# Expert tiles of a routed LSTM layer: the first two tiles' columns made by products with tables of ones, the last tile's rows added by weighted products

## The chip, the cores and the metric

One core of a Trainium2 chip runs the whole program. The time is the device time of one execution in microseconds (us), lower is better. The number compared is the median over runs.

## The reference, cut to what matters

The network has four layers over 625 nodes with 512 features, each a graph part, an attention part and a feed-forward part. The change touches only the last feed-forward part, a mixture of 8 experts of which each row (node) uses 2. Each expert is an LSTM whose sequence has one step here, so it starts from a zero state:

```python
xn = layernorm(x)                                 # 625 x 512
logits = xn @ router_w + router_b                 # 625 x 8
top_vals, top_idx = top_k(logits, 2)
rw = softmax(top_vals, axis=1)                    # two weights a row
for e in range(8):                                # for the rows that chose e
    i, g, o = split(xn @ Wi[e] + b[e])            # the forget gate meets a zero cell
    c = sigmoid(i) * tanh(g)
    y_e = (sigmoid(o) * tanh(c)) @ Wo[e] + bo[e]  # 512 x 512
x = x + sum over the two chosen experts of rw * y_e
```

## The kernel before, in words

All five engines and the DMA queues run one hand-ordered program. PSUM is split into 4 slots of two banks; `TILES` (line 146 and after) gives the order in which TensorE fills them and says which engine empties each ("A" ScalarE, "V" VectorE). `begin` (line 814) makes TensorE wait until the tile four before has been emptied. `full`, `evacd` and `made` are waits on semaphores: a tile filled, a tile emptied, a value made.

**Routing.** VectorE normalises the rows (L1771), TensorE transposes them, five row blocks of 125 rows (`turn_rows`, L855), ScalarE copies them out (L1440), and `router` (products on L824) makes the logits. VectorE adds the bias (L1959), subtracts the maximum (L1963), waits for ScalarE's exponential (L1487), and picks the two best experts (`pick2`, L1928 to L1944). TensorE counts the rows per expert with a triangular table and tables of ones (L1364, L1366, L824, float32: two records per product in the profile). From the counts (read at L2517) VectorE works out for every row its two slots in a list sorted by expert, in which each expert starts on a multiple of 128. The list has EX = 17 tiles of 128 slots, of which each belongs to one expert.

**Filling the tiles.** POOL fetches one weight table by an indirect DMA (L790, 1 MB each: "i", "g", "o" for the three gates and "y" for the output), then writes each row block of xn twice, to its slots in `rows_by_expert` (L797, 10 scatters of 256 KB), then fetches the other tables. Three sets of four tables fit at a time. SyncE waits for all ten scatters, then loads tile 0 and tile 1 (L617). TensorE transposes tile 0 (L1381), VectorE copies it out (L2556). Beside this TensorE transposes the combine weights (L970) and multiplies them with the output biases (L824, 8 rows by 512 columns), and VectorE adds that to X (L2552).

**The loop over 17 tiles.** For tile j TensorE does, in this order: gate i of tile j (a bias product of 24 rows in bf16, L1389, and 4 float32 products of 512 columns, L1393, two records each), the transposes of the hidden rows of tile j-1 (L1400), gate g, the output rows of tile j-1 (L824), the transposes of tile j+1 (L1381), gate o. ScalarE applies sigmoid and tanh, VectorE multiplies and copies (L2568, L2575, L2562). SyncE stores the output rows to `expert_rows` (L620; the last two tiles on L623).

**The end.** When all 17 stores have landed, POOL gathers each row block's two outputs (L807, 10 gathers). VectorE adds them to X, weighted (L2581, L2584), and SyncE writes the result (L627).

## Time and profile before

| | |
|---|---|
| median of three runs | 4341.97 us (4341.44 to 4346.38) |
| the profiled execution, its own time | 4356.8 us |
| its span in the profile | 4354.6 us |
| granted TensorE clock, mean | 0.959 |
| busy: TensorE, VectorE, ScalarE, POOL | 4111.0, 2294.4, 1870.3, 456.7 us |
| the chain that ended last, by engine | TensorE 92%, VectorE 5%, others 1% or less |

Times in the rows are microseconds from the start of the span. A row of the timeline gives start, length, engine, line, operation, output and input, and in brackets the idle time before it and what ended it. Busy time is that of all instructions of an engine in a stretch, overlaps counted once; "PEclk" is the clock that TensorE was granted, 1.00 for 2.4 GHz and 0.50 for 1.2 GHz. "PEld" is the load of the stationary operand. Everything described above begins at about 3990 and is over at 4354.6.

### The profile page before, as it was taken

How to read it: one execution, taken by the hardware profiler on the slowest of the kernel's cores; microseconds unless marked ns; L12 is line 12 of the kernel's file. 1: busy time of each engine (PE TensorE's matmuls, PEld its weight loads, DVE VectorE, ACT ScalarE, POOL GpSimd, SP SyncE). 2: the span in 40 equal slices, each digit the busy share in tenths (PEclk: the TensorE clock that was granted, in tenths of full speed). 3: DMA queues.
4: the chain of work that ended last, by engine and by line, in shares of the span. 5: the costliest groups of instructions: out<-in, count | busy, mean ns of one | idle time of the engine just before them, and what ended most of it. 6: DMA issues, size and time to landing. Idle time of an engine off the chain costs nothing.

```text
span 4354.6 us, 138764 instructions
## 1 busy us (share of the span) xinstructions
PE 4111.0 (94%) x53867; PEld 2286.2 (53%) x53867; DVE 2294.4 (53%) x10677; ACT 1870.3 (43%) x7114; POOL 456.7 (10%) x450
## 2 busy tenths in 40 slices
PE   9888899899999999999999999999999998986897
PEld 7445445455555544456788744434444575455343
DVE  6323512666666666666666666656665153454111
ACT  0010102377777655577777655555554142120111
POOL 0010000100000033100000033201231000011221
PEclk9998899999999999999999999999999998996898
DMA  3000110451000000000000000000000150101874
GB/s 117 17 32 26 39 46 29 146 168 37 10 0 0 1 2 2 5 0 0 0 0 0 1 2 2 5 0 1 2 1 9 58 125 23 65 25 28 328 296 149
DMA packets 65464, 195.72 MB, mean 45 GB/s; under 512 B 30024, under 2 KB 37903, under 8 KB 49387
## 3 DMA queue, kind: packets, MB, share of 16 engines
q0 software_dynamic: 25744, 105.19, 7.6%
q1 hardware_dynamic: 39613, 89.02, 6.2%
q8 instruction: 78, 1.28, 0.1%
q14 instruction: 29, 0.24, 0.0%
HBM read 159.74 MB, written 34.15 MB: 45 GB/s over the span
## 4 chain that ended last, share of the span: by engine, by line
PE 92%; DVE 5%; ACT 1%; issue 1%; POOL 1%; DMA 1%; POOLq 0%; DVEq 0%; ACTq 0%
PE PS L1107 51%; PE PS L824 23%; PE PS L1393 4%; PE PS L1101 3%; PE PS L910 3%; PE PS L1165 2%; PE PS L855 1%; PE PS L1243 1%; PE PS L1293 1%; PE PS L1233 1%; PE PS L1223 1%; ACT BUF L1440 0%; DVE stats L1754 0%; PE PS L883 0%; PE PS L1389 0%
## 5 line engine op out<-in xcount | busy, mean ns | idle before, releaser
L1107 PE MATMUL PS<-BUF,ls_hid 128*1 128x256 f32 x40000 | 2323.0, 379 | 4.8 <-DVE ls_hid L2183 4.7
L1107 PEld LDWEIGHTS PS<-BUF,ls_hid 128*1 128x1 f32 x40000 | 1112.9, 83 | 1004.2 <-DVE ls_hid L2183 289.3
L2153 DVE STREAM_TRANSPOSE ls_turn<-PS 128x192 f32<-128x192 f32 x1250 | 479.2, 383 | 466.9 <-PE PS L1107 466.6
L1559 ACT ACTIVATE ls_th<-ls_pr 128x1 f32<-128x1 f32 x2500 | 601.0, 287 | 102.1
L824 PE MATMUL PS<-ring,BUF 128*125 128x512 f32 (+1 forms) x1120 | 480.6, 588 | 19.5 <-DVE BUF L1895 5.8
L2183 DVE SCALAR_TENSOR_TENSOR ls_hid<-ls_gate,ls_th 128x1 f32<-128x1 f32 x2500 | 345.9, 149 | 233.7 <-ACT ls_th L1559 214.6
L1552 ACT ACTIVATE ls_gate<-ls_turn 128x6 f32<-128x6 f32 x1250 | 265.6, 212 | 319.4 <-DVE ls_turn L2153 239.4
L824 PEld LDWEIGHTS PS<-ring,BUF 128*125 128x125 f32 x1120 | 211.0, 191 | 275.2 <-issue 255.6
L1440 ACT ACTIVATE BUF<-PS 128x500 f32<-128x500 f32 (+1 forms) x100 | 50.8, 562 | 619.7 <-PE PS L855 619.5
L2158 DVE STREAM_TRANSPOSE ls_turn<-PS 128x64 f32<-128x64 f32 x1250 | 279.2, 223 | 0.1
L2164 DVE SCALAR_TENSOR_TENSOR ls_pr<-ls_gate 128x4 f32<-128x4 f32 x1250 | 215.5, 172 | 112.1 <-ACT ls_gate L1552 4.1
L1101 PE MATMUL PS<-BUF,picked 126*1 126x256 bf16 (+1 forms) x5000 | 263.1, 272 | 8.7 <-ACT picked L1569 6.9
L1569 ACT ACTIVATE picked<-pick 128x1 bf16 x624 | 128.5, 206 | 298.4 <-PE PS L1107 277.8
L1554 ACT ACTIVATE ls_gate<-ls_turn 128x2 f32<-128x2 f32 x1250 | 255.7, 205 | 0.2 <-DVE ls_turn L2158 0.2
L2169 DVE SCALAR_TENSOR_TENSOR ls_c<-ls_pr 128x2 f32<-128x2 f32 x1250 | 200.5, 160 | 42.6
L2174 DVE TENSOR_SCALAR ls_gate<-ls_c 128x2 f32<-128x2 f32 x1250 | 217.6, 174 | 0.0
L1564 ACT ACTIVATE BUF<-ls_hid 128x4 f32 x625 | 130.8, 209 | 192.0 <-DVE ls_hid L2183 192.0
L732 POOL DMA_INDIRECT edges_by_cell<-duo x80 | 94.5, 1181 | 890.1 <-DVE ls_turn L2153 887.0
L824 PE MATMUL PS<-BUF,ring 128*128 128x113 f32 (+1 forms) x640 | 181.2, 444 | 2.3 <-ACT BUF L1440 1.4
L1101 PEld LDWEIGHTS PS<-BUF,picked 126*1 126x1 bf16 (+1 forms) x5000 | 124.2, 84 | 98.5 <-ACT picked L1569 7.9
L855 PE MATMUL PS<-ident,BUF 125*128 125x125 f32 x390 | 65.0, 336 | 96.1 <-DVE BUF L1771 80.9
L1165 PE MATMUL PS<-AH,rows 125*32 125x512 bf16 (+3 forms) x2560 | 155.6, 297 | 0.0
(384 smaller groups left out, 3601.9 us busy)
## 6 DMA issues: line engine op xcount, KB each, us to landing
cell_bias<-BUF SPq DMA_DIRECT2D x5, 2441.4 KB
BUF<-cell_bias POOLq DMA_DIRECT2D x5, 2441.4 KB, 14.9
gate_inputs<-BUF SPq DMA_DIRECT2D x5, 1344.0 KB
rows_by_expert<-BUF POOLq DMA_DIRECT2D x1, 4352.0 KB, 29.7
BUF<-rows_by_expert SPq DMA_DIRECT2D x17, 256.0 KB, 7.0
expert_rows<-BUF SPq DMA_DIRECT2D x17, 256.0 KB, 2.3
BUF<-in_L_wh SPq DMA_DIRECT2D x4, 1024.0 KB, 12.6
ring<-in_L_w SPq DMA_DIRECT2D x4, 1024.0 KB, 4.8
```

Source lines behind the costliest of these rows:

```text
L824: ins = nc.tensor.matmul(out, a, b, start=(j == 0), stop=(j == len(terms) - 1))
L1101: nc.tensor.matmul(ls_sum[u][f][32 * q:32 * q + 1, :], picked[0:k, :], gx_tile[g][0:k, q, 2 * f:2 * f + 2, :, :].rearrange("p u j n -> p j ...
L1107: ins = nc.tensor.matmul(ls_sum[u][f][32 * q:32 * q + 1, :].rearrange("p (j n) -> p j n", j=4), ls_hid[:, c:c + 1], ls_half[:, q, c, :, f, :],
L1165: ins = nc.tensor.matmul(PS[p:e, 1, a:b], m[:, p:e], hot_rank[u][:, a:b], start=False, stop=False, skip_group_check=True)
L1552: nc.scalar.activation(ls_gate[:, f, 0:6], ls_turn[:, f, 2:8, 0], ACT.Tanh).then_inc(ls_sig[f], 1)
L1554: nc.scalar.activation(ls_gate[:, f, 8:10], ls_turn[:, f, 0:2, 0], ACT.Tanh).then_inc(ls_out_gate[f], 1)
L1559: nc.scalar.activation(ls_th[:, f, c:c + 1], ls_pr[:, f, c:c + 1], ACT.Tanh, scale=0.5, bias=ls_pr[:, f, 2 + c:3 + c]).then_inc(ls_tanh[f], 1)
L2153: V.transpose(ls_turn[:, f, 2:8, :], ls_sum[u][f][:, 64:256].rearrange("p (g n) -> p g n", g=6)).then_inc(ls_turned[f], 1)
L2158: V.transpose(ls_turn[:, f, 0:2, :], ls_sum[u][f][:, 0:64].rearrange("p (g n) -> p g n", g=2)).then_inc(ls_turned_o[f], 1)
L2164: V.scalar_tensor_tensor(ls_pr[:, f, :], ls_gate[:, f, 0:4], 1.0, ls_gate[:, f, 4:8], ALU.add, ALU.mult).then_inc(ls_prod[f], 1)
L2174: V.tensor_scalar(ls_gate[:, f, 6:8], ls_c[:, f, :], 0.5, None, ALU.mult).then_inc(ls_state[f], 1)
L2183: V.scalar_tensor_tensor(ls_hid[:, 2 * f + c:2 * f + c + 1], ls_gate[:, f, 8 + c:9 + c], 1.0, ls_th[:, f, c:c + 1], ALU.add, ALU.mult).the ...
```

## The change

Five things are altered, all in the last feed-forward part, except for one more blank DMA at the program's start.

1. The router's products are interleaved with the last transposes, and VectorE no longer waits for the exponential before picking.
2. The counts are made in bf16 (0 and 1 are exact), the total counts first.
3. The columns of tiles 0 and 1 no longer come from memory: VectorE compares an iota of 256 columns with each row's two slots, and TensorE multiplies xn by these tables of ones (20 products of 256 columns). The ten scatters stay, for tiles 2 to 16.
4. POOL fetches tables i0, g0, o0 and i1 ahead of the scatters, and g1, y0, o1, y1 behind them.
5. Tile 16's rows are not stored and gathered. Its rows in `expert_rows` are blank from the start, and a weighted table of ones (VectorE, transposed on TensorE) multiplies tile 16's rows in PSUM, in one accumulation with the bias products, which move here from ahead of the loop. POOL's gathers wait only for the stores of tiles 0 to 15.

The core of the diff:

```diff
+                pool.dma_start(ys_d[128 * (EX - 1):128 * EX, :], blank).then_inc(pad_out, 16)
-                pool.wait_ge(ex_routed, 1)
-                fetch("i", 0)
-                pool.wait_ge(ex_routed, 2)
+                pool.wait_ge(ex_ready, 1)
+                for q, j in (("i", 0), ("g", 0), ("o", 0), ("i", 1)):
+                    fetch(q, j)
+                pool.wait_ge(ex_ready, 2)
                 for i in range(2 * NT):
                     pool.indirect_dma_start(xs_d, ...xn[:, i % NT, :], None).then_inc(ex_scattered, 16)
+                for q, j in (("g", 1), ("y", 0), ("o", 1), ("y", 1)):
+                    fetch(q, j)
+                for j in range(2, EX):
...
-                pool.wait_ge(ex_stored[0], 16 * (EX // 2 + 1))
+                pool.wait_ge(ex_stored[0], 16 * (EX // 2))
...
+            def turn_and_route(turned, stage, ready, which, n):
+                for t in range(NT):
+                    if t == NT - 1:
+                        route_row(stage, 0, turned, which, n)
+                    o = begin(turned, t)
+                    ready(t)
+                    for c in range(KC):
+                        ins = nc.tensor.transpose(...)
+                    ins.then_inc(tile_full, 1)
+                for t in range(1, NT):
+                    ins = route_row(stage, t, turned, which, n)
+                ins.then_inc(tile_full, 1)
...
-                nc.tensor.matmul(o[0:R, 0:8 * NT], ltri, hots.rearrange("p t e -> p (t e)"), start=True, stop=False)
+                mm_all(o[:, 512:520], [(ones16, hots16[:, t, :]) for t in range(NT)])
+                nc.tensor.matmul(o[0:R, 0:8 * NT], ltri, hots16.rearrange("p t e -> p (t e)"), start=True, stop=False)
...
+                o = begin("L3f.xa", 0)
+                pe.wait_ge(*made("L3f.place"))
+                for c in range(KC):
+                    ins = mm_all(o[:, 256 * c:256 * c + 256],
+                                 [(xn[:, t, 128 * c:128 * c + 128], ex_first[:, t, :]) for t in range(NT)])
+                ins.then_inc(tile_full, 1)
...
                 for j in range(EX + 1):
                     if j < EX:
-                        pe.wait_ge(*evacd(f"L3f.x{j}"))
+                        pe.wait_ge(*(evacd(f"L3f.x{j}") if j > 1 else evacd("L3f.xa") if j else (ex_ready, 4)))
                         gate("i", j)
...
+                    if j == EX - 2:
+                        turn_probs("L3f.cT", sm[:, 0, :, :], 8)
+                        pe.wait_ge(ex_ready, 5)
+                        o = begin("L3f.pT", 0)
+                        for t in range(NT):
+                            ins = nc.tensor.transpose(o[:, 128 * t:128 * t + R], ex_last[:, t, :], ident[0:R, 0:R])
+                        ins.then_inc(tile_full, 1)
+                for t in range(NT):
+                    o = begin("L3f.b", t)
+                    nc.tensor.matmul(o[0:R, 0:D], combT[:, t * R:(t + 1) * R], eb[:, 0, :], start=True, stop=False)
+                    if t == 0:
+                        pe.wait_ge(*evacd(f"L3f.y{EX - 1}"))
+                    nc.tensor.matmul(o[0:R, 0:D], ex_lastT[:, t * R:(t + 1) * R], ex_y[(EX - 1) % 2],
+                                     start=False, stop=True).then_inc(tile_full, 1)
...
+                for t in range(NT):
+                    st.done(V.tensor_scalar(ex_first[:, t, :], iota[0:R, 0:256], r_slot[:, t:t + 1], None, ALU.is_equal))
+                for t in range(NT):
+                    ins = V.scalar_tensor_tensor(ex_first[:, t, :], iota[0:R, 0:256], r_slot[:, NT + t:NT + t + 1],
+                                                 ex_first[:, t, :], ALU.is_equal, ALU.add)
...
+                dve.wait_ge(*full("L3f.xa", 0))
+                V.tensor_copy(ex_xT[0], both[:, 0, :, :]).then_inc(ex_ready, 1)
+                took(V.tensor_copy(ex_xT[1], both[:, 1, :, :]), "L3f.xa", 0)
+                dve.wait_ge(*evacd("L3f.xa"))
+                for t in range(NT):
+                    for k, dst in enumerate((ex_last, ex_last2)):
+                        at = NT * k + t
+                        st.done(V.tensor_scalar(dst[:, t, :], iota[0:R, 0:128], r_late[:, at:at + 1], r_w[:, at:at + 1],
+                                                ALU.is_equal, ALU.mult))
+                st.after()
+                V.tensor_tensor(ex_last, ex_last, ex_last2, ALU.add).then_inc(ex_ready, 1)
...
                 for t in range(NT):
                     dve.wait_ge(ex_back[t], 32)
+                    for k in range(2):
+                        st.done(V.scalar_tensor_tensor(Xr[:, t, :], ex_got[:, k, t, :], ...))
+                        st.after()
+                    dve.wait_ge(*full("L3f.b", t))
+                    took(V.tensor_tensor(Xr[:, t, :], bank("L3f.b", t)[0:R, :], Xr[:, t, :], ALU.add), "L3f.b", t)
```

## Rows read from the trace of the kernel before

**Rows 1.** Busy time of each engine in three stretches; columns as on the first line.
```profile
core 0: us, PE busy (x) PEld busy (x) DVE busy (x) ACT busy (x) POOL busy (x), PEclk, DMA share, GB/s
4013.00:4043.00 30.00, 8.45 (x10) 2.65 (x9) 4.48 (x12) 0.81 (x1) 23.20 (x22) 0.50 0.78 242
4046.00:4053.00 7.00, 7.00 (x10) 2.63 (x11) 0.00 (x0) 0.37 (x1) 0.14 (x1) 0.57 1.02 421
4073.00:4300.00 227.00, 227.00 (x606) 99.85 (x605) 38.24 (x58) 40.73 (x70) 50.12 (x53) 1.00 0.70 276
```

**Rows 2.** Timeline of the routing, from the router's products to the reading of the counts.
```profile
3995.53 6.89 PE L824 MATMUL PS<-wr,BUF 128*125 128x8 f32 x40 [0.73 <-ACT BUF L1440]
...
4003.49 0.20 DVE L1928 TENSOR_REDUCE smr<-sm 125x5 f32<-125x40 f32 x1 [0.30 <-ACT sm L1487]
...
4006.06 0.20 DVE L1944 TENSOR_TENSOR sm<-sm 125x40 f32<-125x40 f32 x1
...
4008.45 2.28 PE L824 MATMUL PS<-sm,ones 125*128 125x8 f32 x10
...
4010.84 0.22 DVE L2517 TENSOR_TENSOR duo<-PS,iota 128x40 f32<-128x40 f32 x1 [3.66 <-PE PS L824]
```

**Rows 3.** Timeline from the slots to the last scatter and the second table.
```profile
4013.29 0.17 DVE L2544 CAST duo<-duo 125x10 uint32<-125x10 f32 x1
...
4013.41 1.05 POOL L790 DMA_INDIRECT BUF<-in_L_table_i,duo  x1 [27.63 <-DVE duo L2540]
...
4028.23 1.18 POOL L797 DMA_INDIRECT rows_by_expert<-BUF,duo  x1 [0.31 <-issue]
4029.71 0.98 POOL L790 DMA_INDIRECT BUF<-in_L_table_g,duo  x1 [0.30 <-issue]
```

**Rows 4.** Chain of waits, the first gate and pieces of the loop's first turn: start, length.
```profile
4045.93 6.66 PE PS L1393 x8
...
4056.54 0.44 PE PS L1381 x4
...
4060.92 0.32 PE PS L1389
4061.24 3.63 PE PS L1393 x8
```

**Rows 5.** Busy time in two stretches, for the granted clock; columns as in rows 1.
```profile
3993.00:3995.00 2.00, 1.80 (x12) 1.56 (x10) 0.00 (x0) 1.75 (x4) 0.00 (x0) 0.76 0.00 0
...
4017.00:4020.00 3.00, 3.00 (x5) 1.29 (x4) 0.97 (x3) 0.00 (x0) 2.39 (x3) 0.50 0.67 227
```

**Rows 6.** Groups by shape: count, busy us, mean ns of one, idle before.
```profile
L1059 PE MATMUL PS<-duo,BUF 128*125 128x256 f32 x20 | 4.6, 383 | 1.8 <-DVE duo L2053 1.8
L1389 PEld LDWEIGHTS PS<-BUF,duo 24*128 24x128 bf16 x51 | 4.6, 91 | 20.5 <-issue 20.5
L1786 DVE TENSOR_SCALAR BUF<-iota,ids 125x625 bf16<-125x625 f32 x80 | 44.4, 555 | 0.0
L1994 DVE SCALAR_TENSOR_TENSOR BUF<-BUF,sm 125x256 f32<-125x256 f32 x5 | 2.1, 425 | 0.2
```

**Rows 7.** DMA issues at 4013.4, 4028.2, 4029.7 and 4042.3; last number us to landing.
```profile
BUF<-in_L_table_i,duo POOLq DMA_INDIRECT x1, 5.6
...
rows_by_expert<-BUF,duo POOLq DMA_INDIRECT x1, 7.2
...
BUF<-in_L_table_g,duo POOLq DMA_INDIRECT x1, 9.1
...
ring<-in_L_table_y,duo POOLq DMA_INDIRECT x1, 24.1
```

**Rows 8.** Chain of waits at the end: the last store, first gather, last block's first sum.
```profile
4327.94 2.02 DMA expert_rows<-BUF
...
4330.48 1.22 POOL BUF L807
...
4350.33 0.76 DVE X L2581
```

**Rows 9.** Timeline, VectorE's copy of the output rows of tile 15.
```profile
4315.07 0.69 DVE L2562 COPY BUF<-PS 128x512 f32<-128x512 f32 x1 [2.11 <-PE PS L824]
```

More of the change, by code:

```diff
@@ L161 @@
         TILES += [(f"L3f.o{_j}", 1, "A", 8)]
+    if _j == EX - 2:
+        TILES += [("L3f.cT", 1, "A", 8), ("L3f.pT", 1, "A", 8)]
+TILES += [("L3f.b", NT, "V", 8)]
 MADE = [
@@ L612, in _ @@
             sp.wait_ge(ex_scattered, 16 * 2 * NT)
-            for j in range(EX + 1):
+            for j in range(2, EX + 2):
                 if j < EX:
-                    if j >= 2:
+                    if j >= 4:
                         sp.wait_ge(*full(f"L3f.x{j - 2}", 0))
@@ L965, in router, with route_row @@
                 ins.then_inc(tile_full, 1)
+            def turn_and_route(turned, stage, ready, which, n):
[5 more added lines that the diff above has]
+                    for c in range(KC):
+                        ins = nc.tensor.transpose(o[:, c * R:(c + 1) * R], xn[:, t, 128 * c:128 * c + 128], ident[0:R, 0:R])
+                    ins.then_inc(tile_full, 1)
+                for t in range(1, NT):
+                    ins = route_row(stage, t, turned, which, n)
+                ins.then_inc(tile_full, 1)
+            def route_row(stage, t, turned, which, n):
+                o = begin(stage, 0) if t == 0 else slot(stage, 0)
+                pe.wait_ge(*evacd(turned, t))
+                return mm_all(o[0:R, n * t:n * t + n], [(xnT[:, c, t * R:(t + 1) * R], wr[:, which, c, 0:n])
+                                                        for c in range(KC)])
             def turn_probs(stage, a, n):
@@ L1721, in _ @@
                         expert_gate("o", j, ex_o, ACT.Sigmoid)
+                    if j == EX - 2:
+                        copy_probs("L3f.cT", 8)
+                        act.wait_ge(*full("L3f.pT", 0))
+                        took(nc.scalar.activation(ex_lastT.rearrange("p (t n) -> p t n", t=NT),
+                                                  slot("L3f.pT", 0)[:, 0:640].rearrange("p (t n) -> p t n", t=NT)[:, :, 0:R],
+                                                  ACT.Copy), "L3f.pT", 0)
         @block.vector
@@ L2543, in _ @@
                 st.after()
-                V.tensor_copy(ex_at, r_slot).then_inc(ex_routed, 1)
-                V.tensor_scalar(ex_pick[:, 0:EX], r_expert[0:24, :], lane8[0:24, :], None, ALU.is_equal).then_inc(ex_routed, 1)
+                V.tensor_copy(ex_at, r_slot).then_inc(ex_ready, 1)
+                for t in range(NT):
+                    st.done(V.tensor_scalar(ex_first[:, t, :], iota[0:R, 0:256], r_slot[:, t:t + 1], None, ALU.is_equal))
+                for t in range(NT):
+                    st.after(st.n - NT + 1)
+                    ins = V.scalar_tensor_tensor(ex_first[:, t, :], iota[0:R, 0:256], r_slot[:, NT + t:NT + t + 1],
+                                                 ex_first[:, t, :], ALU.is_equal, ALU.add)
+                    if t < NT - 1:
+                        st.done(ins)
+                    else:
+                        make(ins, "L3f.place")
+                V.tensor_scalar(ex_pick[:, 0:EX], r_expert[0:24, :], lane8[0:24, :], None, ALU.is_equal).then_inc(ex_ready, 1)
                 for k in range(2):
                     st.done(V.tensor_tensor(r_pick[:, k, :, :], comb, sm[0:R, 2 + 3 * k, :, :], ALU.mult))
+                st.done(V.tensor_scalar(r_late, r_slot, -128.0 * (EX - 1), None, ALU.add))
                 st.after()
                 st.done(V.reduce_sum(r_w, r_pick.rearrange("p k t e -> p (k t) e"), AX_X))
-                for t in range(NT):
-                    dve.wait_ge(*full("L3f.b", t))
-                    took(V.tensor_tensor(Xr[:, t, :], bank("L3f.b", t)[0:R, :], Xr[:, t, :], ALU.add), "L3f.b", t)
+                st.after()
                 def turned_x(j):
```

85 lines of the change are left out of this document (39 added, 46 removed), and 5 rows, old and new, of tables (MADE, TILES).

## The prediction

> **What bounds it now.** Read first the busy time by stage [rows 1]: TensorE fills every microsecond of 4073 to 4300, the loop over the 17 expert tiles, but of the 30 us ahead of its first product it is busy 8.45, at half clock, and the first gate's 7 us also run mostly at half (mean 0.57). So the loop is a block of fixed length. This change can only move its start and shorten what follows its end. Then the timeline [rows 2, 3] and the chain of waits [rows 4] show what sets the start: router products until 4002.42, two dozen 0.2 us steps of VectorE, the counts, 10 scatters issued by POOL one after the other, the last at 4028.23, its landing 7.2 us later [rows 7], the load of the rows and their transposes; the first gate's last product ends at 4045.93 + 6.66 = 4052.59. At the end [rows 8, 9] the last tile goes to memory, then POOL issues 10 gathers 1.5 us apart, and the last sum can start only at 4350.33, 19.85 us after the first issue.
>
> A difference under 0.2% (8.7 us) counts as no change.
>
> **The routing.** (a) The router now interleaves with the last transposes: TensorE's 0.73 us of idle time ahead of it goes [rows 2]: 0.7. (b) VectorE does not wait for the exponential before it looks for the maxima: the 0.30 us [rows 2] falls to the usual 0.03: 0.27. The wait moves behind the choice of experts, where the exponential is 2 us old. (c) The counts. Before: VectorE starts its mask sum at 4006.06 and can read the counts at 4010.84. The 10 records with tables of ones take 2.28 us, 0.23 each, and there are 20 such records, since float32 takes two a product. In bf16 it is 10 records; a bf16 weight load of 128 columns takes 0.09 [rows 6], at half clock I take 0.11, so 1.15 us, 0.1 ahead and 0.25 behind: the counts can be read 0.2 + 1.5 = 1.7 us after the mask sum starts, instead of 4.78. Gain 3.1. The combine weights (four steps of 0.2 us) fit beside that, so nothing is exposed. Bounds: 1.5 if the small products cost as much as now each, 3.4 if the pass is free. Sum of (a) to (c): 4.1 us.
>
> **The first tile.** Before, scatter, load, transpose. Now the slots stand ready at 4013.46 - 4.1 = 4009.36 [rows 3] and VectorE builds the table: 5 comparisons of 256 columns (a comparison of 625 against the iota takes 0.555, so 0.3 each; 1.5) and 5 comparisons with a sum (256 columns, two inputs: 0.425 to 0.46 [rows 6]; 2.3). Ready at 4013.2, TensorE at 4013.3. Then 20 products of 256 columns in float32, two records each; a record at mostly full clock takes 0.23 [rows 6], so 9.2 us at full and 18.4 at half clock. The engine comes out of idle time, so how long it stays at half decides. The transposes of this stage were already above half in the window 3993 to 3995, some 2.5 us after their start at 3991 [rows 5], the first gate only at 4052, 6.7 us after its start. I take the middle, 4.6, each costing half: 9.2 + 2.3 = 11.5, between 10.4 and 12.6. Products end at 4024.8; VectorE copies tile 0 first (0.1 + 0.7), gate 0 starts at 4025.7. If the clock holds over that 0.9 us gap, the gate's last product ends 0.32 + 3.63 later [rows 4], at 4029.6, against 4052.59: **23.0 us**. If the clock falls in the gap, 1.7 less, and with the table 0.8 us quicker, as much more. What needs weights: POOL now issues four tables first (4009.3, then 1.28 apart as its rows at 4029.71 and after), the first landing 5.6 us after issue [rows 7], the others 2.8 apart: 4015, 4018, 4020, 4023, all ahead of need. VectorE's new 11 operations (the last tile's weighted table, 3.5 us in all) stand between the two copies and the first cell product, which waits for gates 0 that end 8 us later: nothing.
>
> **The second tile and the loop.** The transposes of tile 1 leave the loop: -0.44 [rows 4]. In its last but one turn come the weights' transposes and those of the last tile's table, 5 each, 0.11 each at full clock: +1.1. Their copies on ScalarE (an estimate of 0.7 each, by VectorE's copy of 128x512 in 0.69 [rows 9]) stand ahead of gate 16's, which ends 4 us later; hidden by that gate, and 1.4 us if it were gone. Net +0.7.
>
> **The tail.** Gathers no longer wait for tile 16's store but for tile 15's. VectorE copies tile 15 at 4315.07 to 4315.76 [rows 9]; with the store's 2.02 and the 0.52 to the first issue [rows 8] POOL starts at 4318.3 instead of 4330.48, 12.2 us earlier. The last pair has landed at 4318.3 + 19.85 = 4338.2. Two sums (0.76 each [rows 8], 1.54 with the gap) and the new addition from PSUM (0.7 like the copy [rows 9], and a signal) end at 4340.5, against 4350.33 + 1.54 = 4351.87: **11.4 us**. The products that replace the load stay just inside: tile 16's copy ends at 4327.92; from there, per row block, 2 records of 8 rows and 2 of 128, 512 columns, 0.454 each (an eighth of 3.63): 1.8 us at full clock, so block 4 is there at 4336, wanted at 4339.7. Slack 3.6. VectorE before that: 2.3 us a block from 4327.9, never the later one. The five additions of the bias to X ahead of the loop lay beside the scatters; their going brings nothing. The blank written at the program's start and three small fills lie beside 100 us of TensorE: nothing.
>
> Here a rule and a row part. The row: from 4017 to 4020 TensorE was busy without a break, with products of 8 rows, and the granted clock stayed at 0.50 [rows 5]. In the tail half the records are of that kind. The Trainium skill, TensorE: Matmul & The Clock Gate, Part 1, says that sustained activity of the engine releases the throttle, and names no kind of product that would not count. By the rule the tail's products run at full clock and the sum stands; by the row they could run at half and block 4 would come at 4343.5, and the sum would be 3.8 smaller. I keep full clock, because the other half of the records fills all 128 rows.
>
> **Sum.** 23.0 - 0.7 + 11.4 = 33.7 us. The profiled execution took 4356.8 (span 4354.6 and 2.2 around it): 4323.1. It stands 14.8 above the median of 4341.97; the same difference gives **4308**.
>
> **Rivals.** (A) The queue. Scatters now stand behind three more tables than before. The rows: g0, issued at 4029.71, landed 9.1 later at 4038.8, and the eleventh after the first table, issued at 4042.26, 24.1 later at 4066.4 [rows 3, 7]: they land in order of issue, 2.76 us apart over ten steps. The last scatter is issued at 4027.9, about as now, since 4.1 us won meet 3.85 us of three more issues. If it lands at 4035.4 as now, g1 comes at 4038.9 (needed 4042.2), y0 at 4042, i2 at 4050.8 (needed 4053.7): slack 3 us. Three tables ahead are 8.3 us of transfer against 4.1 us of earlier start and the 22% of the DMA engines' time left free from 4013 to 4043 [rows 1], 6.6 us: just absorbed. If not, up to 4 us go: 4309 to 4312. Chance 0.15. The Trainium skill, DMA: Bandwidth & Descriptors, Queues, rings and completion order, has each engine take its descriptors in ring order, which is what makes this a rival and not a sharing; by it the tables of tile 1 cannot overtake a scatter, and the same 4312 is its worst case. The order of landing above agrees. (B) The tail's products at half clock: 4312, chance 0.12. For it the row at 4017; against it the 128-row half. (C) The new products do not warm the clock, whatever in them were to blame: 18.4 us instead of 11.5, and the gate starts cold (+2.7): 9.6 us lost, 4318, chance 0.06. (D) The other side: the added weight loads and small transposes, or the earlier start, leave the loop at half clock. The place is 4073 to 4300, now at 1.00 throughout [rows 1]. A tile is four times 8 records (14.5 us at 3.63), two or three sets of transposes and three bias products, some 16 us of work, and as much is lost if it runs at half clock. It decides from 34 us of loss, a little over two tiles; three would give 4308 + 48 = 4356. Nothing in the trace ran busy at half for so long with 128-row products. Chance 0.02. (E) The change doesn't do what it says, the first gate still waiting for the scatters through some semaphore: only the tail and the routing gain, 4326; by the code gate 0 waits for the copy alone. Chance 0.01.
>
> **The numbers.** The forecast has 0.64: 4308, of its own from 4305 (clock up early, 1.1; quick table, 0.8; quick counts, 0.3) to 4311 (clock up late 1.1, a fall in the gap 1.7). With A and B and the spread of 5 us between the runs of before the range is 4303 to 4316; C, D, E and what exceeds it are under 2 in 10. Faster by over 0.2%: all but D and a margin, 0.96; within 0.2%: 0.02; slower: 0.02.
>
> **What would show it.** Right: counts read 1.7 us after the mask sum; 40 records of 256 columns in 10.4 to 12.6 us; gate 0 at 4025 to 4027 at clock 1.0 and no pause of TensorE up to gate 2; the first gather at about 4296 (4318.3 less the 22.3 us by which the loop ends earlier); the last sum ready 22 us after the first gather. Wrong: TensorE waiting for a table or for tile 2's rows in the first two turns (A), a wait of VectorE for the last block's products (B), 18 us of new products (C).

## The result, and the profile of the kernel after

The change makes the kernel faster: 4309.11 us (median of 4 runs, 4308.24 to 4320.32) against 4343.32 us (median of 4, 4341.44 to 4346.38) in the same job, a ratio of 0.9927 (95% interval 0.9912 to 0.9943). In a second job (that of runs 9 to 11) the two medians were 4320.08 us (6 runs) and 4353.01 us (11 runs), and the ratio was again 0.9927 (0.9916 to 0.9939). The prediction was 4308 us, in a range of 4303 to 4316. One execution of the kernel before (4841.92 us, mean clock 0.828) and one of run 6 (14719.01 us, mean clock 0.383) were in a slow state and are in none of the ratios.

| | before | after |
|---|---|---|
| the profiled execution, its own time | 4356.8 us | 4308.24 us |
| its span | 4354.6 us | 4306.5 us |
| granted TensorE clock, mean | 0.959 | 0.968 |
| busy: TensorE, VectorE, ScalarE, POOL | 4111.0, 2294.4, 1870.3, 456.7 us | 4099.4, 2298.7, 1869.9, 458.9 us |
| start of the last row normalisation | 3990.38 | 3977.83 |
| from there to the end of the span ("the stretch") | 364.22 us | 328.67 us |

The two spans differ by 48.1 us, and this isn't the change. 12.55 us of it stand ahead of the last row normalisation, in stages that are the same in both programs. These stages show two levels. The granted clock over 3450 to 3500 is 0.76 in some executions and 0.90 in others, and those at 0.76 reach the last normalisation 9 to 13 us later. Both levels occur with the same program: a second profile of the kernel after (run 11) was at 0.76, began its last normalisation at 3990.93 and had a span of 4319.6 us, 35.0 less than the kernel before at the same level. Its stretch was again 328.67 us; spans are printed to 0.1 us. So kernels are compared here by the stretch: 364.22 - 328.67 = **35.55 us** gained, where the prediction's sum was 33.7. The medians differ by 34.2 us in the first job and by 32.9 in the second.

Where it went, by stages, each from the start of the last normalisation or the end of the stage before:

| stage | before | after | gained | predicted |
|---|---|---|---|---|
| to the CAST of the slots | 22.91 | 16.95 | 5.96 | 4.1 |
| to the end of gate 0 | 39.30 | 19.30 | 20.00 | 18.9 |
| the loop, to the copy of tile 15 | 262.48 | 263.11 | -0.63 | -0.7 |
| the tail | 39.53 | 29.31 | 10.22 | 11.4 |

The timeline of the kernel after, from the normalisation to gate 0. The columns are as in the timelines of before, to which it answers [rows 2, 3]:

```profile
3977.83 2.37 DVE L1817 TENSOR_SCALAR BUF<-X,mv,nw 125x512 f32<-125x512 f32 x5
3978.52 3.31 PE L982 MATMUL PS<-ident,BUF 125*128 125x125 f32 x16 [19.37 <-DVE BUF L1817]
...
3982.93 4.95 PE L832 MATMUL PS<-wr,BUF 128*125 128x8 f32 x32
...
3987.98 0.20 DVE L2005 TENSOR_TENSOR sm<-PS,rows 125x40 f32<-125x40 f32 x1 [7.78 <-PE PS L832]
...
3991.12 0.20 DVE L1990 TENSOR_TENSOR duo<-sm 125x40 bf16<-125x40 f32 x1
...
3991.42 0.27 PE L832 MATMUL PS<-duo 125*128 125x8 bf16 x5 [3.55 <-issue]
...
3991.66 0.57 PE L1391 MATMUL PS<-duo 125*125 125x32 bf16 x4
...
3992.33 0.22 DVE L2565 TENSOR_TENSOR duo<-PS,iota 128x40 f32<-128x40 f32 x1
...
3994.78 0.17 DVE L2592 CAST duo<-duo 125x10 uint32<-125x10 f32 x1
...
3996.23 2.05 DVE L2597 SCALAR_TENSOR_TENSOR BUF<-iota,duo,BUF 125x256 f32<-125x256 f32 x5
...
3998.43 10.59 PE L832 MATMUL PS<-BUF 125*128 125x256 f32 x40 [6.21 <-DVE BUF L2597]
...
4010.08 0.37 PE L1415 MATMUL PS<-BUF,duo 24*128 24x512 bf16 x1 [1.05 <-DVE BUF L2623]
4010.38 3.70 PE L1419 MATMUL PS<-BUF 128*128 128x512 f32 x8
...
4013.74 1.63 POOL L804 DMA_INDIRECT rows_by_expert<-BUF,duo  x1 [0.30 <-issue]
...
4015.67 0.98 POOL L796 DMA_INDIRECT BUF<-in_L_table_g,duo  x1 [0.30 <-issue]
```

Gate 0 (L1415 and L1419) starts 1.05 us after the first tiles' products, and waits for the copy alone. The last scatter is issued only while gate 0 runs, at 4013.74. From the mask sum (L1990) to the reading of the counts (L2565) it is 1.21 us, where it was 4.78 [rows 2]. The busy time of the same kernel by stretch answers to [rows 1, 5]: columns as there, PEclk the third number from the end.

```profile
3979.00:3981.40 2.40, 2.40 (x13) 2.40 (x12) 1.20 (x3) 1.29 (x3) 0.00 (x0) 0.50 0.00 0
3981.50:3984.80 3.30, 3.30 (x33) 3.30 (x32) 0.00 (x0) 1.55 (x3) 0.00 (x0) 1.00 0.00 0
3985.00:3988.00 3.00, 2.87 (x14) 2.78 (x14) 0.02 (x1) 0.00 (x0) 0.00 (x0) 0.50 0.00 0
3998.40:4001.90 3.50, 3.47 (x8) 2.86 (x9) 0.56 (x5) 0.00 (x0) 2.58 (x4) 0.50 0.92 382
4002.00:4009.00 7.00, 7.00 (x33) 5.84 (x31) 0.00 (x0) 0.00 (x0) 5.75 (x5) 1.00 0.99 374
4014.00:4280.00 266.00, 266.00 (x711) 117.05 (x711) 43.17 (x65) 49.57 (x85) 61.97 (x65) 1.00 0.72 287
4287.60:4298.20 10.60, 10.56 (x21) 2.89 (x20) 7.18 (x10) 0.00 (x0) 7.72 (x6) 1.00 0.72 199
```

TensorE is busy for every microsecond from 4014 to 4280 at full clock: no wait for a table or for tile 2's rows. The last transposes and the router's small products had the full clock for 3.4 us and then lost it while TensorE stayed busy. The new products of 256 columns began at half and had the full clock from about 4002 on. The chain of waits at the end (start, length, what) answers to [rows 8, 9]:

```profile
4277.19 0.70 DVE BUF L2619
...
4277.91 2.00 DMA expert_rows<-BUF
...
4279.94 0.02 POOLq L812
4279.96 0.96 issue
4280.92 1.22 POOL BUF L815
...
4288.46 1.72 POOL BUF L815
...
4295.35 6.14 DMA BUF<-expert_rows,duo
...
4301.51 0.76 DVE X L2648
...
4303.08 0.69 DVE X L2652
```

The chain still ends in the gathers, not in the products that took tile 16's place. But the first gather comes 1.0 us after the store has landed, where it was 0.5 before. The DMA landings of the last scatter and of table g1, the two on which rival A hung (last number: us from issue to landing; issued at 4013.74 and 4015.67), answer to [rows 7]:

```profile
rows_by_expert<-BUF,duo POOLq DMA_INDIRECT x1, 9.4
...
BUF<-in_L_table_g,duo POOLq DMA_INDIRECT x1, 10.1
```

### The profile page after: what moved, and what is told of

The parts are those of the page before. It is cut to its first block, busy times and chain, and to the rows that moved or that the text cites. A ratio compares the mean times of both kernels' runs of the same rounds, so it can differ in the third digit from the quotient of the medians.

```text
span 4306.5 us, 138862 instructions
## 1 busy us (share of the span) xinstructions
PE 4099.4 (95%) x53904; PEld 2077.4 (48%) x53904; DVE 2298.7 (53%) x10699; ACT 1869.9 (43%) x7115; POOL 458.9 (11%) x452
## 4 chain that ended last, share of the span: by engine, by line
PE 92%; DVE 5%; ACT 1%; issue 1%; POOL 0%; DMA 0%; POOLq 0%; DVEq 0%; ACTq 0%
PE PS L1134 51%; PE PS L832 23%; PE PS L1419 4%; PE PS L1128 3%; PE PS L918 3%; PE PS L1192 2%; PE PS L1270 1%; PE PS L863 1%; PE PS L1320 1%; PE PS L1260 1%; PE PS L1250 1%; ACT BUF L1481 1%; DVE stats L1800 0%; PE PS L891 0%; PE PS L1415 0%
## 5 line engine op out<-in xcount | busy, mean ns | idle before, releaser
L1134 PEld LDWEIGHTS PS<-BUF,ls_hid 128*1 128x1 f32 x40000 | 943.3, 83 | 1167.6 <-DVE ls_hid L2230 298.1
L1128 PE MATMUL PS<-BUF,picked 126*1 126x256 bf16 (+1 forms) x5000 | 250.8, 272 | 8.7 <-ACT picked L1610 6.9
L1128 PEld LDWEIGHTS PS<-BUF,picked 126*1 126x1 bf16 (+1 forms) x5000 | 111.7, 84 | 110.9 <-ACT picked L1610 7.9
L737 POOL DMA_INDIRECT edges_by_dst<-duo x80 | 94.5, 1181 | 526.7 <-issue 310.9
L1192 PE MATMUL PS<-AH,rows 125*32 125x512 bf16 (+3 forms) x2560 | 143.3, 297 | 0.0
## 6 DMA issues: line engine op xcount, KB each, us to landing
BUF<-cell_bias POOLq DMA_DIRECT2D x5, 2441.4 KB, 14.8
```

The source lines that it names most:

```text
L1128: nc.tensor.matmul(ls_sum[u][f][32 * q:32 * q + 1, :], picked[0:k, :], gx_tile[g][0:k, q, 2 * f:2 * f + 2, :, :].rearrange("p u j n -> p j ...
L1134: ins = nc.tensor.matmul(ls_sum[u][f][32 * q:32 * q + 1, :].rearrange("p (j n) -> p j n", j=4), ls_hid[:, c:c + 1], ls_half[:, q, c, :, f, :],
L1192: ins = nc.tensor.matmul(PS[p:e, 1, a:b], m[:, p:e], hot_rank[u][:, a:b], start=False, stop=False, skip_group_check=True)
```

## The experiments

All are edits of the kernel after. "Stretch" is that of one profiled execution. It tells cases apart where the time of a run does not, but not below some tenths of a microsecond: the tail alone, from the copy of tile 15 to the end, took 28.90 to 29.31 us in the seven runs whose edits leave it alone and whose last sum waits for no product (1, 3, 4, 6, 7, 8, 11).

| run | edit | time of the profiled run, or median where the runs are counted | stretch | against 328.67 |
|---|---|---|---|---|
| 1 | counts in float32 | 4314.22 | 332.16 | +3.49 |
| 2 | transposes first, then the router | 4313.27 | 331.96 | +3.29 |
| 3 | products between counts and first tiles | 4309.10 | 328.19 | -0.48 |
| 4 | products ahead of the transposes | 4308.50 | 327.02 | -1.65 |
| 5 | last tile through memory | 4325.74 (4 runs) | 338.62 | +9.95 |
| 6 | first two tiles through memory | 4339.34 (10 runs) | 348.18 | +19.51 |
| 7 | one table ahead of the scatters | 4328.00 | 337.41 | +8.74 |
| 8 | six tables ahead | 4308.31 | 328.45 | -0.22 |
| 9 | sums after all gathers | 4327.81 | 335.97 | +7.30 |
| 10 | 3 and 4 together, five tables, waits swapped | 4316.86 (6 runs) | 324.68 | -3.99 |
| 11 | none | 4320.08 (6 runs) | 328.67 | 0.00 |

**1. The counts in float32.**

```diff
-        ltri, ones16 = duo[0:R, 384:448].bitcast(BF16)[:, 0:R], duo[0:R, 448:512].bitcast(BF16)
-        hots16 = duo[0:R, 939:959].bitcast(BF16).rearrange("p (t e) -> p t e", t=NT)
+        ltri, ones16 = duo[0:R, 384:384 + R], ones[0:R, :]
+        hots16 = sm[0:R, 4, :, :]
```

> The changed kernel with its counts made in float32 again, in the new order. The measure is the stretch from the start of the row normalisation (first of the five 125x512 tensor scalars of the last layer) to the end of the span: 328.7 us in the changed kernel, 364.2 before. Theory: the count's passes are wholly exposed, so mask sum to first reading grows from 1.21 to 4.8 us and the stretch by 3.6 to 332.3. Rival: the combine weights and POOL's queue set that time anyway, and the stretch grows by 1 or less.

The stretch became 3.49 us longer, and the timeline shows why:

```profile
3993.53 0.20 DVE L1989 TENSOR_TENSOR sm<-sm 125x40 f32<-125x40 f32 x1
...
3993.83 2.27 PE L831 MATMUL PS<-sm,ones 125*128 125x8 f32 x10 [3.54 <-issue]
...
3998.31 0.22 DVE L2564 TENSOR_TENSOR duo<-PS,iota 128x40 f32<-128x40 f32 x1 [3.66 <-PE PS L1390]
```

4.78 us from the mask sum to the reading, as in the kernel before, and the first five products are 10 records in 2.27 us here, 5 records in 0.27 us in bf16. The type alone accounts for the term of the counts.

**2. The router after all transposes.**

```diff
-                turn_and_route("L3f.xnT", "L3f.lg", lambda t: pe.wait_ge(*made("L3f.xn", t + 1)), 3, 8)
+                turn_rows("L3f.xnT", xn, lambda t: pe.wait_ge(*made("L3f.xn", t + 1)))
+                pe.wait_ge(*evacd("L3f.xnT"))
+                router("L3f.lg", xnT, 3, 8)
```

> The changed kernel with the router's products behind all transposes again. Theory A: the idle 0.73 us lay inside the short time at full clock, so the interleaving gave back 2.0 us (first transpose to last router product 9.4 against 11.35), and the stretch grows by 2.0 to 330.7. Theory B, as in the prediction: only the idle 0.73 us counts, the stretch grows by 0.7 and the rest of the 2.0 was chance of the clock's phase.

```profile
3980.23 3.73 PE L863 MATMUL PS<-ident,BUF 125*128 125x125 f32 x20 [19.37 <-DVE BUF L1819]
3984.70 6.88 PE L832 MATMUL PS<-wr,BUF 128*125 128x8 f32 x40 [0.73 <-ACT BUF L1483]
...
4002.13 11.29 PE L832 MATMUL PS<-BUF 125*128 125x256 f32 x40 [6.21 <-DVE BUF L2599]
...
4305.23 2.07 PE L1467 MATMUL PS<-BUF 128*125 128x512 f32 x2
4307.40 0.69 DVE L2654 TENSOR_TENSOR X<-PS,X 125x512 f32<-125x512 f32 x1 [0.67 <-PE PS L1467]
```

Transposes and router take 3980.23 to 3991.58, 11.35 us against 9.37 in the kernel after: the 2.0 us of the first theory. Only 0.73 of them is idle time of TensorE. The rest is clock: in both orders the full clock is granted for 3.4 us, and with the idle time inside it 25 records pass (2.57 us busy in the 3.30 us from 3994.0 on in the kernel before) where the interleaved order passes 33 in as long. The eight others then run at half clock, at about 0.2 us each: 1.6 of the 2.0 us by this estimate. The other 1.3 us of this run are not the router's: the first tiles' products got their clock later (11.29 us, +0.7), and in the tail it fell to half, so that VectorE waited 0.67 us for the last block. That is rival B, in an execution of another kernel: two records take 2.07 us at half and 1.12 at full clock. It occurs, and costs 0.7 us, not 4, because the clock fell only at 4297.2, with five of the ten pairs of records done.

**3. Products between the counts and the first tiles.** Three products of 512 columns, their results overwritten.

```diff
+                for _ in range(3):
+                    nc.tensor.matmul(o[:, 0:512], xn[:, 0, 0:128], xn[:, 1, :], start=True, stop=True)
                 pe.wait_ge(*made("L3f.place"))
```

> The changed kernel with three filler products (128 columns of weights, 512 moving columns, float32, result overwritten) on TensorE between the counts and the products with the tables of ones, while it would be idle for 6.2 us. Theory: the clock is at full when the 40 records begin, so they take 9.2 us instead of 10.6; but table g of tile 1 landed only 0.9 us before its use, so the loop then waits 0.5 us for it, and the stretch shrinks by 0.9 to 327.8. Rival A: the tables have room, the whole 1.4 comes out (327.3). Rival B: the fillers do not raise the clock or run over and delay the 40 records: 0 or up to 1 us longer.

```profile
3997.00:3999.80 2.80, 0.85 (x3) 0.17 (x2) 2.80 (x11) 0.00 (x0) 2.19 (x3) 1.00 0.59 193
4000.00:4003.20 3.20, 3.20 (x9) 2.48 (x9) 0.25 (x2) 0.00 (x0) 2.29 (x4) 0.50 0.94 356
4003.30:4009.00 5.70, 5.70 (x28) 5.01 (x28) 0.00 (x0) 0.00 (x0) 4.55 (x4) 1.00 0.98 387
```

The clock came up during the three products, but they ended at 3997.67, and TensorE stood idle for the 1.95 us until the tables were ready at 3999.63. The full clock outlasted the idle time and was lost 0.2 us after the new products had begun. They took 10.59 us, as without the extra work, where the theory had 9.2. The first gate ended 36.16 us after the normalisation, against 36.25; the other 0.4 of the -0.48 us lie in the tail, within its spread.

**4. Products ahead of the last transposes.** Four of 512 columns.

```diff
+                o = begin("L3f.xnT", 0)
+                pe.wait_ge(*made("L3.done"))
+                for _ in range(4):
+                    nc.tensor.matmul(o[:, 0:512], ident[:, :], iota[:, 0:512], start=True, stop=True)
                 turn_and_route("L3f.xnT", "L3f.lg", lambda ...)
```

> The changed kernel with four filler products (identity by 512 columns of the iota, float32, overwritten) on TensorE during the last row normalisation, from the end of the residual sums on. Theory: transposes and router run at full clock, 6.3 us instead of 9.4, and since slots, tables and scatters all move along, the whole 3.1 comes out: stretch 325.6. Rival: the clock falls again in the middle, as it does now 3.4 us after it rose, and only 1 us or less comes out; or the fillers run over into the transposes.

Transposes and router fell from 9.37 to 6.92 us, so their clock is worth 2.45 us. But the first tiles' products rose from 10.6 to 11.8 us: half of the gain was given back one stage on. They began 2.4 us sooner, and the clock did not: it came up at 4003.75, 24.1 us after the normalisation, as in the kernel after (4001.92, also 24.1), which is now 5.9 us after their start instead of 3.5. Gate 0 ended 1.24 us sooner; the rest of the -1.65 is in the tail. The theory's 3.1 us for the whole stretch did not come.

**5. The last tile through memory.** Its store, and the gathers' wait for it, are back; the weighted product leaves the accumulation with the bias. The last tile's rows come by the gathers.

```diff
+            sp.wait_ge(*evacd(f"L3f.y{EX - 1}"))
+            sp.dma_start(ys_d[128 * (EX - 1):128 * EX, :], ex_y[(EX - 1) % 2]).then_inc(ex_stored[(EX - 1) % 2], 16)
...
-                pool.wait_ge(ex_stored[0], 16 * (EX // 2))
+                pool.wait_ge(ex_stored[0], 16 * (EX // 2 + 1))
...
-                    nc.tensor.matmul(o[0:R, 0:D], ex_lastT[:, t * R:(t + 1) * R], ex_y[(EX - 1) % 2], start=False, stop=True
```

> The changed kernel with tile 16 stored and gathered as before: SyncE stores it, POOL's gathers wait for it, and the products of its rows in PSUM are left out (the bias products and the making of the weighted table stay). The result is the same sum. Theory: the early start of the gathers is the whole gain of the tail, from VectorE's copy of tile 15 to the end 39.5 us instead of 29.3, so the stretch from the row normalisation grows by 10.2 to 338.9. Rival: the products at the end cost something themselves, so leaving them out gives 2 us or more back and the stretch grows by 8 or less.

Measured: stretch +9.95 us, ratio to the kernel before 0.9951 (0.9933 to 0.9969). The chain of waits of this kernel has the short way from the landing to the first gather again:

```profile
4300.42 2.03 DMA expert_rows<-BUF
4302.45 0.53 issue
4302.98 1.22 POOL BUF L817
```

**6. The first two tiles through memory.** Table of ones, products and copies are out; tiles 0 and 1 are loaded and transposed; only table i0 goes ahead of the scatters. The edit is long, its core is:

```diff
-            for j in range(2, EX + 2):
+            for j in range(0, EX + 2):
...
-                for q, j in (("i", 0), ("g", 0), ("o", 0), ("i", 1)):
-                    fetch(q, j)
+                fetch("i", 0)
...
-                    ins = mm_all(o[:, 256 * c:256 * c + 256],
-                                 [(xn[:, t, 128 * c:128 * c + 128], ex_first[:, t, :]) for t in range(NT)])
+                turn_x(0)
```

> The changed kernel with tiles 0 and 1 scattered, loaded and transposed as before and the fetches in their old order (i0, the ten scatters, the rest); router, counts and tail as changed. Theory: from the cast of the slots to the end of the first gate's last product 39.1 us instead of 19.1, and tile 1's transposes back in the loop, 0.4: the stretch grows by 20.4 to 349.1. Rival: without the 20 products of 10.6 us and with the tables' queue relaxed the loss is clearly smaller, 15 or less.

```profile
4038.25 0.58 PE L1408 MATMUL PS<-BUF,duo 24*128 24x512 bf16 x1 [0.90 <-issue]
4038.76 6.43 PE L1412 MATMUL PS<-BUF 128*128 128x512 f32 x8
```

The first gate ends at 4045.19, 55.67 us after the normalisation against 36.25: 19.42 of the 19.51 us by which the stretch grew. The cold first gate (6.43 us instead of 3.70) is 2.7 of them. The median of this run misleads: its ratio to the kernel before is 0.999 (0.998 to 1.0), 4 us, though its stretch is 16.0 us shorter. Nine of its ten executions lay between 4337.9 and 4341.1, the profiled one at clock 0.76 in 3450 to 3500, the slower level of the stages ahead; the kernel before's were mostly near 4343, some 13 us under its execution at that level (4356.8). At one level the spans are 4354.6 and 4337.7.

Runs 5 and 6 and the gain of the routing add up: 9.95 + 19.5 + 6.0 = 35.5 us, the whole.

**7. One table ahead of the scatters.**

```diff
-                for q, j in (("i", 0), ("g", 0), ("o", 0), ("i", 1)):
-                    fetch(q, j)
+                fetch("i", 0)
...
-                for q, j in (("g", 1), ("y", 0), ("o", 1), ("y", 1)):
+                for q, j in (("g", 0), ("o", 0), ("i", 1), ("g", 1), ("y", 0), ("o", 1), ("y", 1)):
```

> The changed kernel with only table i0 ahead of the scatters, g0, o0 and i1 right behind them. Theory: g0 is then issued at its old distance behind the last scatter, lands 9.1 us later, about 6 us after gate i0's end, TensorE waits there, and nothing gives it back: stretch 328.7 + 6 = 334.6. Rival: the scatters end 4 us earlier, tables and rows of tiles 1 and 2 come earlier too, and as they are what bounds the loop's start the cost is 2 or less.

```profile
4031.53 6.31 PE L1418 MATMUL PS<-BUF 128*128 128x512 f32 x8 [6.10 <-DMA BUF<-in_L_table_g,duo]
```

One row holds the whole answer: 6.10 us of waiting for g0, issued at 4022.23 behind the scatters and landed 9.3 later, and then a gate of 6.31 us instead of 3.70 at a clock that had fallen. 6.10 + 2.61 = 8.71, measured +8.74. The wait was expected, its price in clock wasn't.

**8. Six tables ahead.** g1 and o1 go ahead of the scatters too.

```diff
-                for q, j in (("i", 0), ("g", 0), ("o", 0), ("i", 1)):
+                for q, j in (("i", 0), ("g", 0), ("o", 0), ("i", 1), ("g", 1), ("o", 1)):
...
-                for q, j in (("g", 1), ("y", 0), ("o", 1), ("y", 1)):
+                for q, j in (("y", 0), ("y", 1)):
```

> The changed kernel with g1 and o1 fetched ahead of the scatters too (i0, g0, o0, i1, g1, o1, then the scatters, then y0, y1 and the rest). In the changed kernel table g1 landed 0.9 us ahead of its use, y0 1.6, the rows of tile 2 1.9. Theory: the queue has less than 2 us of room, so two more tables in front (2.5 us of POOL, 5 us of transfer) bring y0 or tile 2's rows late, and TensorE waits 2 to 4 us: stretch 331 to 333. Rival: the room is larger than the landing times say, stretch within 0.5 of 328.7.

No wait of TensorE appeared; the stretch moved by -0.22 us, and the forecast of 2 to 4 us of waiting was wrong. The last scatter was issued 3.0 us later after the normalisation than in the kernel after and landed 7.8 us after its issue. That is not a gain of the order: in the two profiles of the kernel after it took 9.4 and 7.0 us. The order of the tables has some microseconds of freedom from four to six ahead, and none at one.

**9. The sums after all gathers.** VectorE waits for all five pairs before its first sum.

```diff
                 for t in range(NT):
                     dve.wait_ge(ex_back[t], 32)
+                for t in range(NT):
                     for k in range(2):
```

> The kernel after, with VectorE waiting for all five pairs of gathers before its first sum. In the tail of the kernel after three of the ten gather issues took 1.72, 1.55 and 1.51 us instead of 1.19, each within 0.3 us of the start of one of VectorE's sums or while it ran, and the issue of all ten took 14.43 us instead of 13.77. Theory: VectorE's sums lengthen the issue on GpSimd. Then all ten take 1.19 to 1.22 here and the issue 13.8 us, the last pair lands 0.6 us sooner after the first gather, and the stretch is longer only by the sums that now come last: five blocks of 1.54 + 0.03 + 0.69 = 2.3 us, 11.3 us after the last landing instead of 2.3; in all 328.67 + 9.0 - 0.6 = 337.1. Rival: the long issues come from the DMA side or by chance, so two or three of 1.5 to 1.7 stand here too; stretch 337.7.

All ten gathers took 1.19 to 1.22 us, and from the first issue (4293.21) to the last (4306.72) it was 13.51 us instead of 14.43. In the kernel after the three long ones (1.72, 1.55 and 1.51 us) each overlap a sum of VectorE. Run 9 alone doesn't prove the cause, since run 2, with its sums in place, has ten short issues and 13.51 us too. The profiles taken together do, and they show which overlap counts. Two pairs, from the kernel after and from run 11:

```profile
4288.37 1.53 DVE L2648 SCALAR_TENSOR_TENSOR X<-BUF,duo,X 125x512 f32<-125x512 f32 x2
4288.46 1.72 POOL L815 DMA_INDIRECT BUF<-expert_rows,duo  x1 [0.31 <-issue]
...
4301.47 1.57 DVE L2648 SCALAR_TENSOR_TENSOR X<-BUF,duo,X 125x512 f32<-125x512 f32 x2
4301.53 1.19 POOL L815 DMA_INDIRECT BUF<-expert_rows,duo  x1 [0.31 <-issue]
```

In the 13 profiles 21 gather issues took 1.30 to 1.72 us beside a sum. Each began 0.09 to 0.52 us after the start of one of the two sums of a block, and ended 1.06 to 1.07 us after that sum's end: the later it began, the shorter it was. Issues that began before a sum or over 0.6 us into it took 1.19 to 1.20. Nine began 0.04 to 0.10 us into one and took 1.19 all the same, and there the sum took 0.77 to 0.82 us instead of 0.75, as in the second pair. So one of the two waits for the other.

What the long issues cost at the end is another matter. In run 11, the same kernel, the issue took 13.81 us and not 14.43, the last landing 6.74 and not 6.14, and the tail was 29.31 us in both. In run 9 the last landing took 5.56, which makes half of the difference between 337.1 forecast and 335.97; the sums and also the writes of the result, which follow them, no longer ran beside the gathers there, and which of the two matters was not tried.

**10. Clock and waits together.** The products of run 4, five instead of three of run 3, table g1 also ahead of the scatters, and:

```diff
-                pool.wait_ge(ex_stored[0], 16 * (EX // 2))
                 pool.wait_ge(ex_stored[1], 16 * (EX // 2))
+                pool.wait_ge(ex_stored[0], 16 * (EX // 2))
```

> The kernel after with work added on TensorE and two orders changed: 4 products of 512 columns ahead of the last transposes, 5 more between the counts and the first tiles' products (their results are overwritten), the table g of tile 1 also ahead of the scatters, and GpSimd's two waits for the stores in the other order. Theory: 10 records of 512 columns fill the time from the counts to the table (about 6 us), so the clock is up when the first tiles' products begin and stays up: 40 records at 0.23 = 9.2 us instead of 11.8 with the first set of products alone. Gate 0 ends 32.4 us after the start of the last row normalisation instead of 36.25 in the kernel after. With no wait for tables or rows the stretch is 327.0 - 2.6 = 324.4. The order of the two waits: if the later one is the one that costs, the first gather follows the landing of its store after 0.5 us instead of 1.0, and the stretch is 324.0. Rival 1: the clock falls again some 3.4 us after it rose, whatever runs, as it did with three products between counts and table: 10.6 to 11.8 us for the forty records, stretch 325.4 to 326.6. Rival 2: TensorE, now 3.9 us earlier, waits for the rows of tile 2 (0.4 us ahead of need with six tables first, some 1.9 in the kernel after): up to 1.5 us given back. The time of a run carries up to 12 us of scatter from stages that are the same in all, so the median may stand anywhere from 4303 to 4318; beside the kernel after in the same job, 3 to 5 us faster.

```profile
3989.97 7.20 PE L1401 MATMUL PS<-BUF 125*128 125x512 f32 x10
3997.01 8.80 PE L832 MATMUL PS<-BUF 125*128 125x256 f32 x40
4006.86 0.37 PE L1421 MATMUL PS<-BUF,duo 24*128 24x512 bf16 x1 [1.05 <-DVE BUF L2629]
```

```profile
4274.69 2.00 DMA expert_rows<-BUF
4276.69 0.53 issue
4277.22 1.22 POOL BUF L815
```

The 40 records at full clock throughout took 8.80 us, and gate 0 ended 32.74 us after the normalisation (32.4 forecast, 36.25 in the kernel after). The swapped waits bring the first gather back to 0.53 us after the landing. The stretch is 324.68 us, 3.99 under the kernel after, 3.51 of it by the end of gate 0, and TensorE never waited in the loop. The tail was 28.82 us, just under the 28.90 to 29.31 of the runs that leave it alone, so how much of the 0.48 us by which the first gather comes sooner reaches the end is not shown. All six of its runs (4304.61 to 4318.59 us) lie under all six of the kernel after in the same job (4319.84 to 4321.30); the ratios to the kernel before, 0.992 (0.9908 to 0.9932) and 0.9927, overlap. By the profile it is the best of the three kernels; in times its lead, 0.1%, stands on this one job. It buys this with 18 records of TensorE work whose result nobody reads.

**11. The kernel after, again.**

> The kernel after, unchanged, five rounds on the chip of the run before it. It gives the scatter of its own time and its stretch a second time: 328.7 within 0.3. Over the kernel before 0.9925 by the difference of the two stretches (35.6 less of scatter in other stages nothing). If the difference of the profiled spans (48) were the effect, the ratio would be 0.989.

The stretch repeated to the 0.1 us of the spans, and the ratio too; the 48 us between the first two profiles did not.

## Why the prediction was right, point by point

- **(a) The router, 0.7 forecast, 2.0 measured.** The step priced the idle time only. What it missed: the idle time lay inside the few microseconds in which the full clock was granted, when a record of 8 columns takes 0.1 us instead of 0.2. Run 2 gave the 2.0 back in the same stage.
- **(b) The exponential, 0.27 forecast, 0.40 measured** (3.14 us from the bias sum to the mask sum, before 3.54): right in kind.
- **(c) The counts, 3.1 forecast, 3.57 measured.** Run 1 showed the type to be the cause. The price per bf16 record, 0.11 us, was taken from a weight load of 128 columns, and the ten came out at 0.8 us in all.
- **The first tile, 23.0 forecast with the routing, 25.96 measured.** Besides the 1.9 us of the routing, the tables were ready at TensorE 3.5 us after the slots instead of 3.9, and the forty records took 10.6 us instead of 11.5, the clock rising 3.5 us after their start instead of the 4.6 taken as the middle. (The lower bound read the rise under the transposes 2.5 us after their start; 0.76 over 3993 to 3995 puts it at 2.9.) The copy and the gate came 0.2 us dearer. That the clock would hold over the 1 us gap was right: gate 0 ran at 3.70 us. Run 6 showed the parts to be worth 19.5 us beside the routing.
- **The loop, -0.7 forecast, -0.63 measured**, at full clock and busy 266.00 of 266.00 us. Rival D did not come.
- **The tail, 11.4 forecast, 10.2 measured.** Two terms were taken over from the kernel before and came out longer. The landing of the store now ends the second of POOL's two waits and not the first, so the first gather comes about 0.45 us later after it (0.96 and 0.02 against 0.53, undone in run 10). And from the first gather to the last block's first sum it is 20.59 us instead of 19.85. In this profile that lies in the issue (14.43 us instead of 13.77), in run 11 in the last landing (6.74 instead of 6.06), where it is 20.57 in all. The issues are held up by the sums (run 9), but those of the kernel before have sums beside them too; what makes the whole longer is open. That tile 16's products would be ready was right, by 5 us in the kernel after: the last ends at 4298.2, its sum starts at 4303.08. They took 2.1 us a row block and not 1.8, but tile 16's copy came 10.57 us after tile 15's instead of 12.15.
- **Rival A, the queue,** did not come, but its slack was under 1 us at g1, not 3: issued at 4015.67, landed 10.1 us later at 4025.8, and wanted from 4026.4. In run 11 the same table landed 9.1 us after its issue, 1.6 us ahead of need. The last scatter took 9.4 us to land in one profile and 7.0 in the other, and 7.2 in the kernel before, so the three more tables ahead of it don't explain the 9.4. Run 7 showed what a wait there costs, run 8 that the order of tables is not a fine balance.
- **Rival B** was half right. The clock fell under the tail's products in three runs: at 4301.3 in run 1, at 4297.2 in run 2 and at 4293.9 in run 4. It cost 0.7 us in run 2 and nothing in the other two; in run 4 the last product ended 0.2 us before its sum was wanted. So a fall of the clock midway uses up the lead that the products have over the sums, 4.9 us in the kernel after. The forecast's time for this case, 4343.5, was also added up wrong: twice the 8.17 us at full clock from 4327.92 on is 4344.3. The Trainium skill, TensorE: Matmul & The Clock Gate, Part 1, has activity release the throttle. The tail of the kernel after agrees (1.00 over 10.56 of 10.60 us busy). That of run 2 does not by itself: from 4289.6 to 4296.8 TensorE was busy for all 7.20 us, at 1.00, and from 4299 to 4307 for all 8.00 us, at 0.50.
- **Rivals C and E** did not come either: the new products had the full clock 3.5 us after their start, and gate 0 followed the copy by 0.25 us, while the scatters were still being issued.
- **The time.** Errors of +2.96, +0.07 and -1.18 us left 35.55 against 33.7. The absolute time came out at 4309.11 against 4308, nearer than the steps were, and that is luck. The forecast took 14.8 us off for the difference of profile and median in the kernel before, which is the two levels of the stages ahead; with 35.55 in place of 33.7 the same working gives 4306.5, and the mix of levels in the runs put 2.7 us back. The sum of parts was tested by the stretch, not by that 1 us. The range had room for 5 us of such spread in the runs of before; the kernel after's own runs spread by 12, one of the four lies above the range, and so does the second job's median, beside a kernel before that stood higher too.

## What to carry to other kernels

When small products run just after an idle engine, price them by the clock as well as by the gap: a gap of 0.7 us inside the granted stretch cost 2.0, and a wait of 6.1 us cost 8.7. When a wait in one place is moved to another semaphore or to another neighbour, read again the terms that used to be fixed beside it, such as the lag of the first gather behind the store. And when two profiles differ in stages that are the same code, compare from a common mark near the change: here that separated 35.5 us from 48, and showed a gain of 16 where a median showed 4.

## What the runs showed of the hardware that was not expected

- TensorE can lose its full clock while it is busy: from 3981.50 to 3984.80 it was busy for 3.30 of 3.30 us at 1.00, then 2.87 of 3.00 us at 0.50, with the same products of 8 columns. Products of 512 columns ahead of them took 2.45 us off this stage (run 4), yet the rise under the first tiles' products stayed at 24.1 us after the normalisation, although these began 2.4 us sooner.
- An engine's two successive waits are not alike. When the late semaphore is the first waited for, POOL issues 0.53 us after it; when it is the second, 0.98 us (0.02 + 0.96). The late one is the first waited for in the kernel before and in runs 5 and 10 (0.53 in all three), the second in the other ten profiles. Run 10 swapped the two, and its other edits lie over 250 us earlier. Why is open.
- VectorE's sums over two tensors in SBUF lengthen POOL's DMA issues that begin 0.09 to 0.52 us into one, from 1.19 to between 1.30 and 1.72 us, and not those that begin sooner or later (run 9). A gate product of VectorE did so too (one gather of 1.52 us in run 10). The Trainium skill, SBUF — State Buffer, "SBUF: two separate sides", has the port pair that both share held by the one that starts first for its whole instruction, with the other fully blocked. The rows agree: the held issues end 1.06 to 1.07 us after the end of the sum, whatever their start. The excess is at most 0.53 us beside sums of 0.75 us because an issue begins inside the sum and, by 1.19 - 1.06, is held only from about 0.1 us after its start (an estimate).
- Long stages that a change does not touch can have two levels: clock 0.76 or 0.90 over 3450 to 3500, worth 9 to 13 us at the last normalisation, and which is the usual one differs by program and by job, as far as the times tell. What sets the level was not tried.
